# A Mamba layer's products with B on GpSimd: four states to an instruction, in four double ring buffers

## The reference

```python
xz = u @ in_w.T                      # 256 -> 2 x 512
x, z = jnp.split(xz, 2, axis=-1)
x = silu(conv_b + causal_conv4(x))   # four taps
xdbl = x @ xp_w.T
dt = softplus(xdbl[..., :16] @ dt_w.T + dt_b)
Bm, Cm = xdbl[..., 16:32], xdbl[..., 32:]
dA  = exp(dt[..., None] * A)                     # per channel and state
dBx = (dt * x)[..., None] * Bm[:, :, None, :]
h   = dA * h + dBx                               # along the 56 tokens
y   = einsum('bdn,bn->bd', h, Cm) + x * Dp
y   = (y * silu(z)) @ out_w.T
```

## Time and profile before

| | us |
|---|---|
| median of 3 runs | 5985.66 (5982.96 to 5986.95) |
| the profiled execution | 5982.95 |
| its span, first to last instruction | 5981.3 |
| GpSimd busy | 5274.7 (88%) |
| VectorE busy | 5264.1 (88%) |
| TensorE matmuls busy | 5193.1 (87%) |
| ScalarE busy | 3354.3 (56%) |

### The profile page before, as it was taken

How to read it: one execution, slowest core, us unless ns; L and a number is a source line. 1 busy time by engine, 2 the same in 40 slices (tenths; PEclk the granted TensorE clock), 3 DMA queues, 4 the chain that set the end, 5 groups by cost and what they waited for, 6 DMA issues and landing times. The chain is left out here.

```text
span 5981.3 us, 47174 instructions
## 1 busy us (share of the span) xinstructions
PE 5193.1 (87%) x14366; PEld 2599.2 (43%) x14366; DVE 5264.1 (88%) x4001; ACT 3354.3 (56%) x5046; POOL 5274.7 (88%) x2694
## 2 busy tenths in 40 slices
PE   6968898988989888898878898988989888898889
PEld 5824444444444444444334444444444444444344
DVE  3469999999999999999969999999999999999900
ACT  0055666656666565666555666656666565666511
POOL 0069999999999999999969999999999999999900
PEclk9989999999999999999989999999999999999999
DMA  4133323233232322323123323232232322323164
GB/s 154 71 112 96 102 66 108 69 102 91 77 108 63 106 85 85 109 63 105 59 82 99 98 70 108 69 102 87 80 109 63 105 80 91 108 61 108 59 217 141
DMA packets 220338, 563.65 MB, mean 94 GB/s; under 512 B 27842, under 2 KB 94274, under 8 KB 218532
## 3 DMA queue, kind: packets, MB, share of 16 engines
q1 hardware_dynamic: 204276, 533.89, 28.7%
q10 hardware_dynamic: 15808, 26.75, 1.2%
HBM read 500.43 MB, written 60.58 MB: 94 GB/s over the span
## 5 line engine op out<-in xcount | busy, mean ns | idle before, releaser
L909 POOL TENSOR_TENSOR dbx<-dtx,b_all 128x896 f32<-128x896 f32 x1792 | 3705.9, 2100 | 0.2
L665 PE MATMUL mamba_ps<-hc,ident 128*128 128x448 f32 x7168 | 3152.6, 575 | 627.1 <-POOL hc L916 613.6
L735 ACT ACTIVATE mamba_ps<-dt,w 128x448 f32<-128x448 f32 x3584 | 2135.2, 629 | 1617.4 <-DVE hc L848 1298.8
L665 PEld LDWEIGHTS mamba_ps<-hc,ident 128*128 128x128 f32 x7168 | 1376.5, 199 | 2183.1 <-issue 1231.4
L841 DVE TENSOR_TENSOR_SCAN mamba_ps<-mamba_ps,dbx 128x896 f32<-128x896 f32 x1120 | 2254.0, 2013 | 52.8 <-ACT mamba_ps L735 50.7
L916 POOL TENSOR_TENSOR hc<-hc,c_all 128x896 f32<-128x896 f32 x672 | 1409.0, 2097 | 0.0
L841 DVE TENSOR_TENSOR_SCAN hc<-mamba_ps,dbx 128x896 f32<-128x896 f32 x672 | 1353.8, 2015 | 52.5 <-ACT mamba_ps L735 52.0
L848 DVE TENSOR_TENSOR hc<-mamba_ps,c_all 128x896 f32<-128x896 f32 x1120 | 1216.1, 1086 | 77.8 <-DVE mamba_ps L841 2.0
L628 PE MATMUL mamba_ps<-u,w 128*128 128x448 f32 x1792 | 803.0, 574 | 59.0 <-DVE skip L858 25.7
L628 PEld LDWEIGHTS mamba_ps<-u,w 128*128 128x128 f32 x1792 | 363.7, 205 | 437.0 <-issue 336.8
L818 DVE SCALAR_TENSOR_TENSOR x<-mamba_ps,w,x 128x440 f32<-128x440 f32 (+2 forms) x672 | 436.5, 650 | 16.4 <-ACT x L749 15.8
(11 more groups left out here) (95 smaller groups left out, 2182.2 us busy)
## 6 DMA issues: line engine op xcount, KB each, us to landing
b_all<-bc_scratch SPq DMA_DIRECT2D x448, 448.0 KB, 6.6
c_all<-bc_scratch SPq DMA_DIRECT2D x448, 448.0 KB, 6.1
u<-u_scratch SPq DMA_DIRECT2D x58, 448.0 KB, 8.7
y_scratch<-ytok SPq DMA_DIRECT2D x56, 448.0 KB, 3.2
src<-y_scratch SPq DMA_DIRECT2D x56, 448.0 KB, 4.6
xb<-in_x SPq DMA_DIRECT2D x4, 3136.0 KB, 11.8
u_scratch<-ub ACTq DMA_DIRECT2D x28, 448.0 KB, 8.1
src<-in_x SPq DMA_DIRECT2D x28, 448.0 KB, 6.8
```

Source lines behind the costliest of these rows:

```text
L665: last = nc.tensor.matmul(y_ps[j % 2], ident[:, :], hc[g % HC_RING][:, e * T:(e + 1) * T], start=False, stop=(g == GP - 1 and e == 1))
L735: last = nc.scalar.activation(decay[g % 2][:, e * T:(e + 1) * T], blk(dt[s.par], j), ACT.Exp, scale=w[:, c:c + 1])
L909: nc.gpsimd.tensor_tensor(view(dbx[g % BX_RING], 0, [[T, 2], [1, T]]), view(dtx[s.par], j * T, [[0, 2], [1, T]]), view(b_all, 2 * g * T, [ ...
```

## The change

`dbx` becomes four buffers of 4 x 448 columns in place of eight of 2 x 448, in the same amount of memory. `make_dbx` is called for even slots only and multiplies dt*x of block j by four rows of B: one instruction of 1792 columns for slots n and n+1. It raises `dbx_ready` by 2 when it is done, waits for one more scan (n + 2 instead of n + 1), and in the first eight slots for two chunks of B. The scan reads its half of the double buffer through `bx`.

```diff
-        dbx = [sb(f"dbx{i}", 2 * T) for i in range(BX_RING)]
+        dbx = [sb(f"dbx{i}", 4 * T) for i in range(BX_RING // 2)]
...
+        bx = lambda g: pair(dbx[g // 2 % (BX_RING // 2)], g % 2)
...
-                    nc.vector.tensor_tensor_scan(dst, h, dbx[g % BX_RING][:, :], 0.0, ALU.mult, ALU.add).then_inc(scan_done, 1)
+                    nc.vector.tensor_tensor_scan(dst, h, bx(g), 0.0, ALU.mult, ALU.add).then_inc(scan_done, 1)
...
                     if j == 0:
                         pool.wait_ge(b_loaded[g], s.at(16, 16))
-                    pool.wait_ge(scan_done, s.at(SLOTS, n + 1))
-                    nc.gpsimd.tensor_tensor(view(dbx[g % BX_RING], 0, [[T, 2], [1, T]]), view(dtx[s.par], j * T, [[0, 2], [1, T]]),
-                                            view(b_all, 2 * g * T, [[T, 2], [1, T]]), ALU.mult).then_inc(dbx_ready, 1)
+                        pool.wait_ge(b_loaded[g + 1], s.at(16, 16))
+                    pool.wait_ge(scan_done, s.at(SLOTS, n + 2))
+                    nc.gpsimd.tensor_tensor(view(dbx[g // 2 % (BX_RING // 2)], 0, [[T, 4], [1, T]]), view(dtx[s.par], j * T, [[0, 4], [1, T]]),
+                                            view(b_all, 2 * g * T, [[T, 4], [1, T]]), ALU.mult).then_inc(dbx_ready, 2)
...
                     for n in range(SLOTS):
-                        make_dbx(s, n)
+                        if n % 2 == 0:
+                            make_dbx(s, n)
                         if by_pool(n - POOL_LAG) and (n >= POOL_LAG or not s.first):
                             weigh(s, n - POOL_LAG)
```

## The result

The changed kernel takes 6043.39 us (median of 4 runs, 6043.02 to 6047.03), the kernel before 5984.86 (4 runs): ratio 1.0099, 95% interval 1.0082 to 1.0117. It is 58 us slower; 5974 was forecast and 6010 was the upper end. The profiled execution took 6043.02 us, its span is 6041.4, 60.1 more than before.

The account below looks back on a forecast made before the run. GpSimd was taken to bound from about the fifth step, 94.2 us a step against VectorE's 93.6. Steps 5 to 26 gain 2 us, the end 3.5, twice: 11 us off 5985.66, forecast 5974, range 5948 to 6010.

Parts of the forecast that it names:

- VectorE's floor: Rival: VectorE sets the step at 93.6 us if the b7 wait is shorter or double products cheaper; 5952 us, chance 0.30.
- A double product takes 3.93 us: Price of one 1792-column GpSimd product, against 4.08 us for two single ones; sixteen pairs save 2.4 us a step.
- Bubbles at the restarts: GpSimd's queue around dtx, its restart and the next double product: 0.11 + 0.13 = 0.2 us added a step.
- GpSimd waits 2.0 us for b7 in each step: Ahead of the fourth double product: b7 lands 8.0 us after slot 30's C product, only 6.0 us of work between.
- b5: nothing, or 0.1: Wait for chunk b5, behind slot 28's C product: landing after 6.1 us against 6.0 us of work between.
- GpSimd's own ring: GpSimd's work plus chunk waits in a step: 92.1 + 2.0 = 94.1 us, against 94.2 before.
- the wait that outgrows the saving: Rival: the b7 wait makes GpSimd's step longer than 94.2 us; 6003 us at a ring of 94.7, chance 0.28.
- Nothing else: Claim that scans, GpSimd's scan waits and its C products add no time; slot 0's product 1.9 us later is covered.
- Steps 1 to 4: 0: First steps of a pass run at VectorE's pace before and after the change: no gain or loss.
- The end of a pass: 3.5 us: Last step to last sums: VectorE loses 0.9 us of waits and the sums end earlier; 3.5 us gained a pass.
- The start: free: Start of a pass: first pair ends at 363.9, before the first scan at 364.82, which waits for ScalarE; no cost.
- With no constant at all: Far end of the slower rival: a double product of 4.08 us, ring 96.5 us, +94 us.

## Why the prediction was wrong

- *GpSimd bounds the kernel, VectorE's floor lies at 93.6 us a step.* Right: with the chunks on time two kernels end at 5949.5 and 5952.2, where 5952 was forecast for the floor.
- *A double product takes 3.93 us.* Right: 3.93 to 3.94 from start to start. (The 4497 ns that the prediction takes from the Trainium skill, "GPSIMD Engine Reference", section "Elementwise — side-by-side cycle accounting", are given there for an addition of 2048 columns, not for a product; no run here has that length, and the price does not rest on it.)
- *Bubbles at the restarts, 0.2 us.* dtx to its restart 2.17 us (2.15 forecast), and 0.13 before the next double product. Right.
- *GpSimd waits 2.0 us for b7 in each step.* Right in place, cause and size: 2.04.
- *b5: nothing, or 0.1.* Mis-sized: 0.23; the landing and the gap were both put at 6.0 to 6.1 us and the difference rounded down. The work was mis-sized too: 92.0 to 92.1 with its restarts, measured 92.5, since over all steps a double product took 3.944 us and a C product 2.053 in the mean (16 x 0.014 + 12 x 0.013 = 0.4). So GpSimd's own ring is 92.3 + 2.4 = 94.7 and not 94.1, and by these terms alone the case was the third one, the wait that outgrows the saving, from 94.2. At 94.7 that rival gave 6003, which is 40 us short of the measured time. So its terms explain less than a third of the 58 us.
- *"Nothing else ... its C products wait for four slots back: never last."* This is the step that failed. Those margins were read from the kernel before, in which nothing was late. A GpSimd that starts slots 6 to 9 late by 2 us makes slot 4's C product late (8.71 us behind its scan, 7.67 before) and TensorE idle for 2.6 to 4.4 us. In 35 of 44 steps its clock is then at half, the projection and the tap are late, and with them the scans for which GpSimd waits: 0.6 us a step on top of 94.7, 95.3 in all. I had written that slot 4's C product is "the one that VectorE feels", and then added the wait to GpSimd's ring as if nobody gave it back. The time went round through TensorE, ScalarE and VectorE and came back as a second wait. The matmuls that keep TensorE at work show the clock's part; the two kernels without chunk waits show that these set it off; moving slot 4's or slot 17's C product only moves the waits.
- *Steps 1 to 4: 0.* Wrong: 12.6 us in two passes. They run at VectorE's pace only while GpSimd has a lead, and the wait for b7 eats it in step 1 (its window of 96.00 us):

```profile
457.40:553.40 96.00, 83.56 (x218) 40.63 (x217) 91.64 (x69) 59.17 (x89) 92.16 (x33) 0.93 0.29 87
```

- *The end of a pass: 3.5 us.* 1.6 and 0.4. No chunk is loaded in the last step, but its start still waits for b5 and b7 loaded in the step before, and slot 30's C product now comes when its scan allows: 3020.28, behind a wait of 1.59 us.
- *The start: free.* Right: the first scan is at 364.19, released by ScalarE, where it was at 364.82.
- *What would show it.* The text named its own falsifier, that GpSimd waits for anything but b7 "or scans". It waits for b5, which meets it. It also waits for scans, which the text allowed because it had tied them to the floor; here they occur in steps over 93.6 us, where VectorE is held up by TensorE.
- *Two sums at the edges.* With no constant at all the ring comes to 96.3 by the prediction's own terms, not 96.5, since a longer double product also covers more of the wait; and a ring of 94.8 gives 6005, not the 6010 of the range. Neither changes the outcome.

In sums, for both passes: steps 5 to 26, 49.2 us lost where 2 x 2 were to be gained; steps 1 to 4, 12.6 lost where 0 was forecast; ends 2.0 gained of 7.

Left open: how the 30 us beside the 28 divide. 94.7 in place of 94.2 over 52 steps gives 26 of them; the rest, and the steps in which the added matmuls did not keep the clock up, no run separates. Open too is what decides whether the clock falls behind a given idle time.

## What to carry to other kernels

Joining two instructions moves the second one's first use of its inputs forward, and whatever lay between the release of that input's buffer and its first use is no longer cover: count that distance in us against the whole way of the refill (wait, issue, landing), for each input apart. A wait placed on the engine that paces a loop is not paid once: follow the late result to the next engine, ask whether its clock or its queue makes the delay longer, and whether the first engine may run ahead again to make it up. A half clock that costs nothing with a margin of 3.1 us between two engines costs time at a margin of 1.0. Here either remedy, chunks issued earlier or single products where chunks are awaited, turns 1.0% of loss into 0.55 or 0.58% of gain.

## What the runs showed that was not expected

- The same eight matmul records take 3.27 us behind an idle time of 3.46 us and 6.24 behind 4.27, but also 5.98 behind 3.35, and 4.97 behind 2.15 in the kernel before: the length of the idle time alone does not tell whether the granted clock will be 0.50.
- A broadcast transfer of 448 KB took 5.7 us (b5) and 8.0 us (b7) from issue to landing in one step, and with three in place of four others issued behind slot 28's C product b7 comes 1.4 us sooner: what is issued just ahead goes into a landing beside the issue time.
- GpSimd's product of two inputs is nearly all columns: 2.04 us from start to start for 896, 3.94 for 1792, so 0.14 us is all that joining two of them saves.
